# ScalarE's squares of z in front of the root for y2n, in a fused attention and feed-forward kernel

## The reference, cut to what matters

```python
# attention, 16 heads of 8 channels: q, k1, k2, v1, v2 = x + x @ W.T + b, in heads
S1, S2 = k1.T @ v1 / n, k2.T @ v2 / n ;  S12 = S1 * S2
out = (q @ S1 * mean(v2)) * g1 + S12.sum(2) * g2 + (q @ S2 * mean(v1)) * g3 + (q @ S12) * g4
out = layernorm(out) * ln_g + ln_b            # root 1: std1
x   = layernorm(x + out @ Wo.T + bo)          # root 2: std2
# feed forward
h   = relu(x @ w1[0] + b1[0]) ;  y = h @ w2[0] + b2[0]
x2  = layernorm(x + y) * gamma + beta         # root 3: std3, gives y2n
x   = layernorm(x + x2)                       # root 4: std4
```

## Time and profile before

| | us |
|---|---|
| median of 3 runs | 218.47 (216.88 to 219.51) |
| the profiled execution: its time | 216.88 |
| its span, first to last instruction | 215.1 |
| TensorE busy in the span | 195.6 (91%) |
| VectorE busy | 163.5 (76%) |
| ScalarE busy | 127.5 (59%) |
| GpSimd busy | 134.2 (62%) |
| TensorE's mean granted clock, of 1 | 0.986 |

### The profile page before, as it was taken

One profiled execution on the slowest core, in us unless ns is written; L12 is line 12 of the kernel. 1 busy time (PEld: TensorE's weight loads), 2 busy tenths in 40 slices (PEclk: granted clock), 3 DMA queues, 4 the chain that ended last, 5 costly groups with the idle time before them and its releaser, 6 DMA issues.

```text
span 215.1 us, 4255 instructions
## 1 busy us (share of the span) xinstructions
PE 195.6 (91%) x1380; PEld 177.9 (83%) x1380; DVE 163.5 (76%) x477; ACT 127.5 (59%) x383; POOL 134.2 (62%) x173
## 2 busy tenths in 40 slices
PE   7879999999998999899989999899989999899930
PEld 7768998997997889787979999798979998888630
DVE  0155845989868987989688886898697878896895
ACT  3122448455559585766576566947575557867571
POOL 8324650465896569675966489755967397776230
PEclk9999999999999999999999999999999999999995
DMA  5999700000010100110010001010011001011012
GB/s 157 103 292 287 188 0 5 2 0 5 0 49 0 52 2 3 49 50 0 0 52 34 16 3 49 0 53 0 0 52 52 0 0 52 0 50 49 2 50 98
DMA packets 12145, 9.98 MB, mean 46 GB/s; under 512 B 642, under 2 KB 9995, under 8 KB 12123
## 3 DMA queue, kind: packets, MB, share of 16 engines
q1 hardware_dynamic: 11082, 8.53, 12.8%
q0 software_dynamic: 320, 0.85, 2.6%
q10 hardware_dynamic: 720, 0.33, 0.6%
HBM read 5.51 MB, written 4.19 MB: 45 GB/s over the span
## 4 chain that ended last, share of the span: by engine, by line
PE 54%; DVE 18%; ACT 13%; issue 8%; DMA 3%; SPq 2%; DVEq 0%; ACTq 0%
PE down_ps L890 17%; PE up_ps L890 14%; PE prep_ps L890 12%; PE z_ps L890 7%; DVE st L689 5%; ACT res L571 5%; DMA vec_rows<-in_L_ffn_b 3%; PE turn_ps L1010 3%; DVE y2n L694 3%; DVE x1T_lo L826 3%; ACT hT L588 2%; ACT z_sq L549 2%; ACT x1T_hi L638 2%; DVE z_ps L788 2%; PE turn_ps L983 2%
## 5 line engine op out<-in xcount | busy, mean ns | idle before, releaser
L890 PE MATMUL down_ps<-w_sb,hT 128*128 128x128 f32 x496 | 61.1, 277 | 0.1
L890 PEld LDWEIGHTS down_ps<-w_sb,hT 128*128 128x128 f32 x496 | 58.4, 192 | 1.2 <-DVE y2n L694 0.4
L588 ACT ACTIVATE hT<-up_ps,cols 128x512 f32<-128x512 f32 x64 | 41.6, 682 | 3.7 <-PE up_ps L890 3.5
L503 POOL TENSOR_TENSOR x1b<-x,b_rows 128x512 f32<-128x512 f32 x16 | 20.6, 1287 | 19.1 <-DVE x L694 19.1
L890 PE MATMUL up_ps<-x1T_hi,w_hi 128*128 128x512 f32 x64 | 26.5, 414 | 4.1 <-ACT hT L588 4.1
L477 POOL TENSOR_TENSOR y2g<-y2n,gamma_rows 128x512 f32<-128x512 f32 x14 | 17.9, 1279 | 13.4 <-DVE y2n L694 13.4
L571 ACT ACTIVATE res<-y,nb,rstd 128x128 f32<-128x128 f32 x60 | 24.6, 483 | 2.1 <-POOL nb L465 2.1
L890 PE MATMUL up_ps<-x1T_lo,w_hi 128*128 128x512 f32 x64 | 25.5, 398 | 0.0
L890 PE MATMUL up_ps<-x1T_hi,w_lo 128*128 128x512 f32 x64 | 25.2, 395 | 0.0
L549 ACT ACTIVATE z_sq<-z_ps 128x128 f32<-128x128 f32 x64 | 16.9, 272 | 12.3 <-PE z_ps L890 12.3
L694 DVE TENSOR_SCALAR x<-z_ps,st,rstd 128x128 f32<-128x128 f32 x64 | 21.9, 404 | 0.6
(11 more groups left out here) (144 smaller groups left out, 426.1 us busy)
## 6 DMA issues: line engine op xcount, KB each, us to landing
X<-in_L_attn_x SPq DMA_DIRECT2D x8, 512.0 KB, 7.9
out<-res SPq DMA_DIRECT2D x15, 256.0 KB, 2.0
w_sb<-in_L_ffn_w POOLq DMA_DIRECT2D x2, 256.0 KB, 8.4
out<-res SPq DMA_DIRECT2D x2, 128.0 KB, 1.9
w_raw<-in_L_attn_Wv ACTq DMA_DIRECT2D x2, 64.0 KB, 2.7
w_raw<-in_L_attn_Wk SPq DMA_DIRECT2D x2, 64.0 KB, 4.2
bv_rows<-in_L_attn_bv ACTq DMA_DIRECT2D x2, 64.0 KB, 4.4
bo_rows<-in_L_attn_bo ACTq DMA_DIRECT2D x1, 64.0 KB, 4.5
```

Source lines behind the costliest of these rows:

```text
L503: pool.tensor_tensor(x1b2[(s + 1) % 2][:, :, :], x1[:, :, :], rows(b2_rows[:, :]), ALU.add).then_inc(x1b2_out, 1)
L588: act.activation(hT[:, k, :], up_ps[k % len(up_ps)][:, :], ACT.Relu, bias=cols[:, 5 + k:6 + k]).then_inc(relu_out, 1)
L890: return pe.matmul(o, lhsT, rhs, start=start, stop=stop)
```

## The change

In each step ScalarE's squares of z for group n+1 and the root `std1` behind them are issued ahead of the root `std3` of group n-1, where they stood behind it. In the six steps with a preparation only the squares of the first bank (tiles 0 and 1) go ahead; the other two, and `std1`, stay behind `std3`.

```diff
@@ -540,14 +540,17 @@
-            def squares(m):
+            def squares(m, tiles):
 
                 wait(act, r1_out, m)
-                for t in range(TILES):
+                for t in tiles:
                     if t % 2 == 0:
                         wait(act, z_done, m * 2 + (t // 2 + 1))
                     act.activation(z_sq[:, t, :], z_ps[t // 2][:, t % 2 * 256:t % 2 * 256 + C], ACT.Square,
                                    accum_out=z_sum[:, t:t + 1]).then_inc(sq_out, 1)
+
+            def std_z(m):
+
                 wait(act, sq_out, m * TILES + TILES)
                 std(z_sum[:, :], std1, std1_out, 1.0 / C)
 
@@ -595,12 +598,18 @@
+                split = st.prep and st.n > 0
+                if st.nxt:
+                    squares(n + 1, range(2 if split else TILES))
+                    if not split:
+                        std_z(n + 1)
                 if st.prev:
 
                     wait(act, st3_out, n)
                     std(two(st3, 2), std3, std3_out, 1.0 / C)
-                if st.nxt:
-                    squares(n + 1)
+                if split:
+                    squares(n + 1, range(2, TILES))
+                    std_z(n + 1)
```

## The result

The changed kernel takes 228.68 us (median, 227.41 to 230.39), the kernel before 218.53 us (216.88 to 219.51): the ratio is 1.050, 95% interval 1.044 to 1.056. The forecast was 227.5 us, 221.5 to 230. The profiled execution of the changed kernel took 227.41 us with a span of 225.6 us, 10.5 us longer than before in both.

A forecast was written before the change was run, and what follows sets the result against it. VectorE's row behind root 3 was taken to bound the kernel; 1.6 (start) + 6.0 (five pairs) + 0.6 (step 13) + 1.8 (step 14) = 10.0 us later gave 226.9 to 228.5, named 227.5, range 221.5 to 230.

The forecast's parts named there:

- That root 3 sets VectorE's row: VectorE's fixed order behind root 3, through y2n to V_sb and x1, sets the time, not TensorE's row.
- Odd steps, 0.60 us: Steps 1, 3, ..., 13, without preparation: in step 9 root 3's reciprocal 0.60 us late, `turn_x1` 0.24 us later.
- Split steps, 0.96 and 0.61 us: Steps with a preparation: `ak_e`, behind V_sb, starts 0.96 us later in step 8 and 0.61 in step 6.
- Pairs, 1.20 and 1.21 us: Each pair in steps 3 to 12 costs 1.20 us with a Gram matrix, 1.21 without; five pairs, 6.0 us.
- Start, 1.6 us: Steps 1 and 2: late root 3 and x1 make the reciprocal of step 2 come 1.6 us later.
- End, 0.6 and 1.84 us: Step 13 adds 0.6 us; in step 14 root 3 goes behind all squares and root 1, 1.84 us.
- The relu's gain turned into a wait: Step 9: `up`'s fourth block starts 0.76 us earlier, but the whole gain becomes waiting for x1 at `turn_x1`.
- The faster one: Rival, chance 0.10: TensorE's pause at `up` goes and nothing replaces it; 4.1 to 5.3 us gained, 212 us.
- No change: Rival, chance 0.06: VectorE's 4.4 us of pauses in a pair absorb most of the 1.2 us; 215 to 219.
- the half case: Rival, chance 0.10: only one of a pair's two delays is paid; 4 to 6 us, 221 to 223.
- The clock: Rival, chance 0.02: TensorE's clock falls to 1.2 GHz for a tenth of steps 2 to 13; 14 us more, 241.
- Signs that were sized too evenly: Expected waits: `turn_x1` about 1 us for x1, `ak_e` about 1 for V_sb, root 3's reciprocal over 0.9.

The follow-up runs named there:

- the edit that shortens the row: Steps 3, 5, ..., 13: VectorE takes st4's statistics behind root 2's, ScalarE root 4 later; ratio to the kernel before 0.997, or 1.029 when made in the changed kernel.
- the first two experiments: Kernel before with the change only in steps 1, 3, ..., 13: ratio 1.013; with it only in split steps 2, 4, ..., 12: ratio 1.022.

## Why the prediction was right

- **That root 3 sets VectorE's row.** Right, and shown by three kernels that each make it late in other steps (2.8, 4.7 and 1.8 us), and by the edit that shortens the row and takes 3.6 us out of the waits for x1 in the changed kernel (some 4.6 us of its time, 3 to 6).
- **Odd steps, 0.60 us.** The reciprocal waits 0.92 us instead of 0.37, 0.55 us more, and starts 1.50 us after the last product of z (138.54), where 1.54 was said. `turn_x1` follows that product by 147.42 - 138.54 = 8.88 us where it followed by 8.67: 0.21 us later, where 0.24 was said.
- **Split steps, 0.96 and 0.61 us.** `ak_e` follows the product of its step by 128.20 - 123.71 = 4.49 us where it followed by 122.84 - 119.32 = 3.52: 0.97 us. In steps 4 and 6 it waits 0.78 and 0.79 us where it waited 0.17: 0.61 and 0.62.
- **Pairs, 1.20 and 1.21 us.** Without a Gram matrix `ak_e` of steps 2 and 6 lie at 54.94 and 103.18 instead of 53.14 and 99.05, which is 2.33 us for two pairs, 1.17 each. With one it is 1.33 us (25.02 against 23.69): the 0.97 and 0.21 us above, and 0.15 us where TensorE starts again after a wait, since `turn_x1` to the product takes 1.31 us instead of 1.25, and `ak_e` to the next product 8.46 instead of 8.37. The sum had left these 0.15 us out.
- **Start, 1.6 us.** `ak_e` of step 2 is 1.80 us late, of which 0.16 were there at the first `turn_x1` (29.32 against 29.16), before any moved instruction: 1.64 us.
- **End, 0.6 and 1.84 us.** From root 3 of step 13 to the reciprocal of root 3 in step 14 the delay grew from 8.70 us (189.78 against 181.08) to 10.51 us (201.23 against 190.72): 1.81 us.
- **The relu's gain turned into a wait.** Right in the changed kernel (`up` from 4.1 to 0.5 us, `turn_x1` to 10.5 us). Where the relu alone was made early, most of the time went to `down` and little to `turn_x1` (its waits 1.9 us instead of 1.2). One reading was wrong: the pause at `up` was counted in seven of the steps that the change touches, for the rival's price of 4.1 to 5.3 us. There are six, 3.6 us; the seventh is in step 15. The forecast's sum does not use it.
- **The rivals.** The faster one fell. The Trainium skill, "Perfetto Trace Analysis" (Optimization Strategy), says to find the gaps on the most-contended engine and make what they wait for start sooner; followed for TensorE's pause alone, that was worth nothing or 0.8 us here (the relu first; two squares first in the odd steps). Its place was real, though: once x1 came earlier too, taking most of the same pause away was worth about 2.9 us (3.5 less the 0.6 of the edit for x1). No change fell by the result itself, and the half case by the first two experiments: both kinds of step pay. The clock stayed at 1.00 in the pair, and its mean over the span was 0.992 against 0.986, though TensorE's pauses reached 1.75 us.
- **Signs that were sized too evenly.** `turn_x1` waits from 0.86 to 1.75 us, where about 1 us was said for all; `ak_e` waits 0.80 us and not about 1 (or 1.2); and the reciprocal of root 3 waits 0.52 or 0.53 us in steps 2, 4 and 6, under the 0.9 that was said. The sum uses how late each comes, not how long it waits, and is not touched.

## What to carry to other kernels

On an engine that works in order, issue the instructions in the order in which their inputs arrive: two squares ahead of a root cost nothing where the root's input is still on its way (ScalarE idled 1.43 us there), and delay the root by 1.34 us in step 8, where its input has arrived (125.51 is 1.80 us after the step's first product, 119.78 was 0.46 after it). Before a pause of the busiest engine is removed, follow each engine's row to its next meeting with the others and write down by how much the second-latest arrival is early (here 0.40 us or nothing for x1, and 0.1 us for the last relu where only the first was moved): the removal wins no more than that. Where two waits end almost together, test the edits for both at once, since each alone will look worthless (0.8 and 0.6 us, together 3.5).

## What the runs showed of the hardware that was not expected

A TensorE that has waited starts a little slower than one that runs on: the four transposes of `turn_x1` are 0.66 us long behind a wait and 0.60 without one, and the four small products of `ak_e` 0.71 and 0.61. Over a pair of steps with two such waits it came to 0.15 us, which no count of instructions shows.

A second wait on ScalarE ahead of root 3, met long before, went with a later start: in step 9 of the kernel changed in step 14 alone the root's reciprocal waits 0.42 us where it waited 0.37, and TensorE's pause behind it is 0.67 us instead of 0.61.
